# Two row buffers, raw rows for the router, and a new order on all engines

## The reference

```python
# attention by Fourier transforms, per sequence
n = layernorm(x)
s = sigmoid(norm(n)); for _ in range(10): s = 3.9 * s * (1 - s)
q = n * (1 + 0.1 * (s - 0.5)) * (1 + 0.1 * wave)
Q, K, V = q @ Wq.T + bq, mem @ Wk.T + bk, mem @ Wv.T + bv     # mem = context * constant
QKV = hamilton(hamilton(fft(Q) * filt, fft(K) * filt), fft(V) * filt)
x = x + ifft(QKV).real
# mixture of experts, top 1 of 8, capacity 1024 each
t = _layer_norm(layernorm(x), ln_gamma, ln_beta)              # a second norm inside
logits = t @ gate_weight.T
e = argmax(logits); weight = softmax(logits)[e]; rank = count of earlier tokens with the same e
x = x + layernorm(x) + weight * (gelu(t @ wi[e]) @ wo[e])     # the last term only where rank < 1024
```

## Time and profile before

| | |
|---|---|
| median of three runs | 3796.45 us (3789.59 to 3796.98) |
| profiled execution, span | 3811.8 us; the page gives no other time for it |
| TensorE busy | 3526.2 us (93%) |
| VectorE busy | 2585.9 us (68%) |
| ScalarE busy | 1623.2 us (43%) |
| GpSimd busy | 1367.9 us (36%) |
| first stage | 0 to 2357 us |

### The profile page before, as it was taken

How to read it: one execution, slowest core, us unless ns; L and a number is a source line. 1 busy time by engine, 2 the same in 40 slices (tenths; PEclk the granted TensorE clock), 3 DMA queues, 4 the chain that set the end, 5 groups by cost and what they waited for, 6 DMA issues and landing times. The chain is left out here.

```text
span 3811.8 us, 50226 instructions
## 1 busy us (share of the span) xinstructions
PE 3526.2 (93%) x15048; PEld 2654.4 (70%) x15048; DVE 2585.9 (68%) x4270; ACT 1623.2 (43%) x2726; POOL 1367.9 (36%) x2985
## 2 busy tenths in 40 slices
PE   6999998998999989989999985999999999999998
PEld 4666666666666666666666653888888888888886
DVE  5888888878888888888888883444444444444443
ACT  4445445535445445445445433333333333333332
POOL 5654654654655645555556541000000000000000
PEclk8999999999999999999999995999999999999999
DMA  6321211121111211211211102333333333333321
GB/s 213 127 97 44 80 64 44 67 77 44 71 62 44 87 58 44 97 58 44 78 67 44 67 34 78 110 105 129 121 112 122 111 122 111 111 103 108 121 101 45
DMA packets 223355, 326.29 MB, mean 86 GB/s; under 512 B 36832, under 2 KB 102624, under 8 KB 223232
## 3 DMA queue, kind: packets, MB, share of 16 engines
q1 hardware_dynamic: 207904, 307.97, 23.4%
q0 software_dynamic: 15360, 16.99, 1.3%
HBM read 256.82 MB, written 101.97 MB: 94 GB/s over the span
## 5 line engine op out<-in xcount | busy, mean ns | idle before, releaser
L1257 ACT ACTIVATE act<-hid_ps 128x512 f32<-128x512 f32 x256 | 153.3, 599 | 802.1 <-PE hid_ps L1188 802.1
L1149 POOL TENSOR_TENSOR tally<-tally,unit 1x1 f32<-1x1 f32 x16 | 2.9, 180 | 1356.7 <-DVE mixed L1330 1356.7
L403 PE MATMUL pair<-w_q,q_spec 128*128 128x512 f32 x1024 | 480.3, 619 | 0.8 <-ACT q_spec L570 0.8
L1318 DVE CAST act_h<-act 128x512 fp32r<-128x512 f32 x256 | 109.4, 428 | 527.8 <-ACT act L1257 527.8
L1188 PE MATMUL hid_ps<-tok_h,w_h 128*128 128x512 f32 x1024 | 406.0, 397 | 2.5 <-DVE tok_l L1306 2.3
L1188 PE MATMUL hid_ps<-tok_l,w_h 128*128 128x512 f32 x1024 | 399.9, 391 | 0.0
L1188 PE MATMUL hid_ps<-tok_h,w_l 128*128 128x512 f32 x1024 | 399.4, 390 | 0.0
L1204 PE MATMUL out_ps<-w_l,act_h 128*128 128x512 f32 x1024 | 398.5, 389 | 0.0
L1202 PE MATMUL out_ps<-w_h,act_h 128*128 128x512 f32 x1024 | 398.3, 389 | 0.0
L1203 PE MATMUL out_ps<-w_h,act_l 128*128 128x512 f32 x1024 | 398.3, 389 | 0.0
L1312 DVE TENSOR_TENSOR w_l<-w_raw,w_h 128x2048 fp32r<-128x2048 f32 x128 | 293.4, 2293 | 90.4 <-ACT w_h L1251 90.4
(11 more groups left out here) (174 smaller groups left out, 8116.2 us busy)
## 6 DMA issues: line engine op xcount, KB each, us to landing
w_raw<-in_L_ffn_wi SPq DMA_DIRECT2D x128, 512.0 KB, 3.4
w_raw<-in_L_ffn_wo SPq DMA_DIRECT2D x128, 512.0 KB, 4.9
w_raw<-in_x SPq DMA_DIRECT2D x32, 1024.0 KB, 5.3
w_raw<-in_ctx SPq DMA_DIRECT2D x32, 1024.0 KB, 7.3
x_res<-in_x SPq DMA_DIRECT2D x31, 1024.0 KB, 5.2
out<-x_res SPq DMA_DIRECT2D x31, 1024.0 KB, 4.2
slots<-x_tok SPq DMA_DIRECT2D x4, 4160.0 KB, 20.5
got<-slots SPq DMA_DIRECT2D x16, 1040.0 KB, 7.5
```

The source lines that it names most:

```text
L403: last = nc.tensor.matmul(pair[k % 2][:, s, :], spec[:, c, tile * 256 + s * P:tile * 256 + (s + 1) * P], w[:, c, :], start=(c == 0 and n = ...
L1149: nc.gpsimd.tensor_tensor(tally[:], tally[:], unit[:], ALU.add).then_inc(tallied, 1)
L1257: nc.scalar.activation(act32[i % 2][:], hid_ps[i % 2][:], ACT.Gelu).then_inc(gelu, 1)
L1318: v.tensor_copy(act_h[i % 4][:], act32[i % 2][:]).then_inc(ah_ready, 1)
```

## The change

1. `rows` and `slot_i` become two buffers each (p = 0 and 1 by the parity of b), with two scatter semaphores. `x_tok` and the step `tokens` go.
2. Since p must be known when the program is written, the loops of TensorE, ScalarE, GpSimd and VectorE take two sequences a turn (SyncE's does not).
3. The router turns the raw `rows`. The gate has its column mean taken out (`gate_m`, in the set-up), so that a row's own mean drops out of the product, and the row's scale (number DIM + 2 of the row) is multiplied onto the logits in `choose`, as one more step.
4. The order changes on all four engines. The turn of tile t waits for the adds of that tile, not for the norm's scales. 

```diff
-            rows = sb("rows", [P, ROWT, ROW])
-            x_tok = sb("x_tok", [P, ROWT, DIM])
+            rows = [sb(f"rows{i}", [P, ROWT, ROW]) for i in (0, 1)]
+            empty = rows[1][:, 0:1, :]
-            slot_i = sb("slot_i", [P, ROWT], i32)
+            slot_i = [sb(f"slot_i{i}", [P, ROWT], i32) for i in (0, 1)]
+            TILE_DONE = (3, 7, 4, 8)
...
TensorE
-                    def turn(b, t, f1_done):
-                        pe.wait_ge(tok_ready, b * 4 + t + 1)
+                    def turn(b, p, t, f1_done):
+                        pe.wait_ge(unfold, b * UNF + TILE_DONE[t])
...
+                    for c in range(CB):
+                        last = nc.tensor.matmul(odd_ps[:, 0:EXPERTS], ones32, gate_g[:, c, :], start=(c == 0), stop=(c == CB - 1))
...
-                    def batch(b, back, ahead):
+                    def batch(b, p, back, ahead):
                         project(b, 3)
                         if back:
                             inverse(b - 1, 0)
                         project(b, 4)
                         if back:
                             inverse(b - 1, 1)
+                        project(b, 5)
                         if ahead:
                             dft(b + 1, c_fold, cf_ready, 0)
                             dft(b + 1, q_fold, qf_ready, 4)
-                        project(b, 5)
...
-                            project(b + 2, 1)
+                            project(b + 2, 1, (0,))
                         if back:
                             logits(b, 2)
                             logits(b, 3)
                         if ahead:
+                            project(b + 2, 1, (1,))
                             project(b + 2, 2)
...
+                    with pe.Fori(3, BATCH - 3, 2) as b:
+                        batch(b, 1, True, True)
+                        batch(b + 1, 0, True, True)
...
ScalarE (the order in a batch before, and after)
-  q_of(b+1); real_parts 2, 3, 4 of b; spectra_c(b+1) with sum_x(b+2); sum_x2(b-1);
-  spectra_q(b+1) with square_x2(b-1) and square_x(b+2); real_parts 5; tokens(b-1); token_blocks 0, 1;
-  context_high(b+1); real_parts 0 of b+1; token_blocks 2, 3; base_of(b-1); real_parts 1; exps
+                        real_parts(b, 2)
+                        real_parts(b, 3)
+                        if ahead:
+                            q_of(b + 1)
+                        real_parts(b, 4)
+                        if back:
+                            sums_x2(b - 1, 1 - p)
+                        real_parts(b, 5)
+                        if ahead:
+                            spectra_c(b + 1, *([(square_x2, b - 1, 1 - p)] if back else []))
+                            context_high(b + 1)
+                            spectra_q(b + 1, *([(sum_x, b + 2)] if ahead2 else []))
+                        else:
+                            squares_x2(b - 1, 1 - p)
+                        if ahead2:
+                            squares_x(b + 2)
+  (then as before: token_blocks 0, 1; real_parts 0; token_blocks 2, 3; base_of; real_parts 1; exps)
...
GpSimd
-                        if ahead:
-                            mean1(b + 1)
                         if router:
                             mean2(b - 2)
-                            stats2(b - 2)
+                            stats2(b - 2, p)
                         if ahead:
+                            mean1(b + 1)
                             stats1(b + 1)
...
VectorE
-                            wait(dve, scattered, b * 64)
-                            wait(dve, base_ready, b * 4)
-                        lo, hi = rows[:, t, 0:DIM], rows[:, t + 2, 0:DIM]
+                            wait(dve, scattered[p], (b - p) * 32)
+                            wait(dve, base_ready, (b - 1) * 4)
+                            if p:
+                                dve.wait_ge(slots_clear, 64)
+                        lo, hi = rows[p][:, t, 0:DIM], rows[p][:, t + 2, 0:DIM]
...
+                        dve.wait_ge(stat2, b * STAT2 + STAT2)
...
+                        a2 = rows[p][:, :, DIM + 2:DIM + 3]
+                        ro.step(v.tensor_tensor(logit[:], lg, a2.broadcast_to([P, ROWT, EXPERTS]), ALU.mult)); ro.wait()
+                        ro.step(v.tensor_tensor(logit[:], logit[:], <gate_c, broadcast>, ALU.add)); ro.wait()
...
-  convert 2; folds_q(b+1); add_attended(b-1, 0); hamilton 2; convert 3; add_attended(b-1, 1); back_to_parts 0;
-  convert 4; hamilton 4; folds_c(b+2); convert 5; hamilton 5 with context_low(b+1) inside; convert 0 of b+1;
-  back_to_parts 1; convert 1 of b+1; choose(b-1); first product of b+1 with place(b-1) inside
+                        convert(b, 2)
+                        hamilton(b, 2)
+                        if back:
+                            add_attended(b - 1, 1 - p, 0)
+                        convert(b, 3)
+                        if ahead:
+                            folds_q(b + 1)
+                        convert(b, 4)
+                        if back:
+                            add_attended(b - 1, 1 - p, 1)
                         wait(dve, inv_mm, b * 4)
                         back_to_parts(b, 0)
-                        convert(b, 4)
                         hamilton(b, 4)
+                        convert(b, 5)
+                        hamilton(b, 5)
+                        back_to_parts(b, 1)
+                        hc.end()
+                        if ahead:
+                            context_low(b + 1)
                         if ahead2:
                             folds_c(b + 2)
...
                         if ahead:
                             convert(b + 1, 0)
+                        if back:
+                            choose(b - 1, 1 - p)
                         if ahead:
                             convert(b + 1, 1)
+                            first_product(b + 1, (lambda: place(b - 1, 1 - p)) if back else None)
```

More of the change, by code:

```diff
@@ L546, in square_x, with sum_x2, square_x2 @@
                         square_sum(b, t, x_in, neg1, square1, (stat1, b * STAT1 + 1), sums1, unused[0])
[L548 to L557, removed]
+                    def sum_x2(b, p, t):
+                        row_sum(b, t, rows[p], sum2, (unfold, b * UNF + UNF), (stat2, b * STAT2), sums2, unused[1])
+                    def square_x2(b, p, t):
+                        square_sum(b, t, rows[p], neg2, square2, (stat2, b * STAT2 + 1), sums2, unused[1])
                     def q_of(b):
@@ L570, in spectra @@
                             nc.scalar.activation(spec[:, u, :], xt_ps[u % 2][:], ACT.Copy).then_inc(f1_ev, 1)
-                            for step, b_ in between:
-                                step(b_, u)
+                            for step, *of in between:
+                                step(*of, u)
                     def context_high(b):
@@ L587, in real_parts, with base_of @@
                         nc.scalar.activation(re_buf[k % 2][:], pair[k % 2][:, 0, :], ACT.Copy).then_inc(re_ready, 1)
-                    def tokens(b):
+                    def base_of(b, p):
                         act.wait_ge(stat2, b * STAT2 + STAT2)
-                        wait(act, logit_mm, b * 4)
-                        act.wait_ge(slots_clear, 64)
                         for t in range(ROWT):
[L594 to L603, removed]
+                            nc.scalar.activation(residual(b)[:, t, :], rows[p][:, t, 0:DIM], ACT.Identity,
+                                                 bias=rows[p][:, t, DIM + 5:DIM + 6],
+                                                 scale=rows[p][:, t, DIM + 4:DIM + 5]).then_inc(base_ready, 1)
                     def token_blocks(b, tiles):
@@ L623, in spectra_q, with sums_x, squares_x, sums_x2 @@
                         spectra(b, q_spec, 4, (f2_mm, b * 6 - 2), between)
-                    all_tiles(0, sum_x, square_x)
+                    def sums_x(b):
+                        for t in range(ROWT):
+                            sum_x(b, t)
+                    def squares_x(b):
+                        for t in range(ROWT):
+                            square_x(b, t)
+                    def sums_x2(b, p):
+                        for t in range(ROWT):
+                            sum_x2(b, p, t)
+                    def squares_x2(b, p):
+                        for t in range(ROWT):
+                            square_x2(b, p, t)
+                    sums_x(0)
+                    squares_x(0)
                     spectra_c(0)
@@ L725, in stats1, with stats2 @@
                         c.end()
-                    def stats2(b):
+                    def stats2(b, p):
                         c = s2c
```

181 lines of the change are left out of this document (87 added, 94 removed).

## The result

The changed kernel takes **3757.9 us** (median of 4 runs, 3753.1 to 3759.0); the kernel before, run beside it, took 3793.4 (3789.6 to 3797.0). The ratio is 0.9886, interval 0.9858 to 0.9913: 35.5 us gained where 122 were forecast. 3757.9 lies outside the range of 3615 to 3722.

The account below looks back on a forecast made before the run. Bound: the ring of waits, with inverse 1 behind add 0 behind hamilton 2. 41.87 + 24.84 = 66.7 us per batch, plus 0.7 for clock, 67.4; 103 plus 19 at the end, 122 off 3796.5, gives 3674 us; range 3615 to 3722.

Parts of the forecast that it names:

- 66.7 us at full clock: First stage, per batch: TensorE's 41.87 us plus 24.84 from real-row copy to first add, without slow clock.
- 67.4 us per batch: First stage: 66.7 us plus 0.7 for a slow-clock loss of 1.4 us taken in half the batches.
- the price of nothing for the doubled loops: Loops unrolled by two: the forecast time held no instruction-fetch cost; such stalls appeared only in rivals.
- Rivals 1 and 2: Slow clock behind inverse 1 in every batch, 21 us more, 3695 (0.15); VectorE fetch stall, 35 us, 3709 (0.12).
- Rival 2: VectorE's branch back, on the ring: a fetch stall of about 2.5 us per pass, 35 us, 3709; chance 0.12.
- hamilton 2: VectorE's product, now ahead of the first add: 8.63 us of the 24.84 leading to inverse 1.
- The experts' loop fetches without a wait at its seam: Argument against rival 2: the experts' loop fetches instructions on each pass, yet shows no wait at its branch.
- Rival 5: VectorE's doubled body, 34 KB in four 8 KB pieces, refetched each pass: 11.6 us, 3836, slower; chance 0.07.
- the ring: First stage's closed chain of waits through TensorE and VectorE, from inverse 1 to the next: 66.7 us per batch.
- The q_spec waits: TensorE waits for q spectra: 0.7 us in front of the q-product, 0.3 inside dft q, 1.0 together.
- Rivals 3, 4 and 5: TensorE bounds at 63.8, 3566 (0.07); scatter wait only moves, 3796 (0.06); whole VectorE body refetched, 3836 (0.07).
- the 5.8 us wait goes: VectorE's wait per batch for the previous rows' scatter, before the first add, vanishes with two rows buffers.

Follow-up runs that it names:

- the mend of the third: Changed kernel with conversion 3 and the first add ahead of hamilton 2, plus ScalarE's row sums put behind the c spectra: 4014.7 us, ratio 1.0566.
- the early add: Changed kernel with conversion 3 and the first add ahead of hamilton 2: 3780.9 us; with VectorE's loop also written out: 3753.5 us.
- the versions of the old order: Changed kernel, old orders, q_of behind real part 2, folds_q behind first add, VectorE's loop written out: 3579.1 us; x's squares also behind the q spectra: 3561.7 us.

## Why the prediction was wrong

**Where the 122 us went.** Between the two profiled executions lie 3811.8 - 3756.6 = 55.2 us: 30 x (70.84 - 69.68) = 34.8 by the batches (103 forecast), 1551.6 - 1525.7 = 25.9 behind the first add of sequence 30 (19 forecast), and 5.5 lost before the first batch (0 forecast). The profiled execution of before lay 17 us above the median of its runs, 3796.45 (its span of 3811.8 against runs whose spans are 1.8 below their times), that of after at its median. The forecast was taken off the median, as if after's execution would lie as high, so these 17 us are part of the miss: 68 + 5.5 - 7 + 17 = 84 = 3758 - 3674. The 68 are the step to explain.

**The step that failed** is the one from "66.7 us at full clock" to "67.4 us per batch", and the price of nothing for the doubled loops. Rivals 1 and 2, weighed at 0.15 and 0.12 and taken one at a time, came together:
- *Clock.* "I take it in half of the batches, 0.7." Each batch had its slow stretch and lost 1.6 to 2.1 us by it. The wait that decides was laid out at 2.9 us and called in between; it was 3.3 to 5.1, and with VectorE's loop written out, at 3.1, each batch still had its stretch. Measured alone: 45 us, for the 21 allowed.
- *Fetch.* Rival 2 put 2.5 us per pass on VectorE's branch. The trace shows 1.7 to 2.0 us of idle there, and writing the loop out gives 3.2 per pass, 41.5 us, since hamilton 2 and the slow stretch grow behind it and the written-out steps are shorter. "The experts' loop fetches without a wait at its seam" was true of TensorE; I carried it to VectorE, which no row covered. Rival 5's size of the body does not hold either: written out, VectorE brings one packet of 8 KB per batch (24 in 1700 us), where 236 instructions at 71 bytes (131072/1840; the working has 73) would bring two.

Together they are 30 x (69.68 - 67.21) = 74 us, of which 21 were in the forecast: 53 of the 68. The other 15 are the ring itself, 67.21 measured at full clock and without the branch where 66.7 were laid out. The Trainium skill, "Runtime: NRT & Kernel Launch", section "Instruction fetch mechanics", says that a branch taken to a page not held stalls until it is fetched; this case agrees, for VectorE's body of two batches (1.67 us idle, packets on q14) and not for its body of one (neither, before and with one buffer).

**What held.** The ring, to 0.5 us a batch. Of its terms, hamilton 2 was low, 8.96 (1037.35 to 1046.31) and 9.32 in place of 8.63, which also makes the wait at inverse 1 longer: it now runs beside GpSimd's real bins. The q_spec waits, 0.8 and 0.2 for 0.7 and 0.3. No scatter wait, none for x_tok; VectorE waits for the logits and real part 1, and also, which was not forecast, for real part 0 (34 waits for real parts in 17 batches). Slow stretches only at inverse 1. Rivals 3, 4 and 5 fell: TensorE is not the bound, no other wait took over the 5.8 us whole, and the fetch is far from 11.6 us a pass.

**What the working did not ask.** It gave the gain to the second buffer ("the 5.8 us wait goes") and took the new order as given. Both runs with one buffer show that wait gone too, in either order, once the turns read raw rows; in the old order 110 us of gain are that part's. The new order gives 109 us back, because it puts hamilton 2 ahead of three things: the first add (inverse 1), conversion 3 (project 5), and the last of the rows (ScalarE's sums and, behind them, the c spectra). I had named the first as the bound, rightly, but as the only one. Taken away one after the other, each gave way to the next, and the mend of the third met a fourth, GpSimd's mean. In the old order conversion 3 is behind hamilton 2 as well, but project 5 stands behind both dfts there and does not wait; the 22.0/18 = 1.2 us of that trace stand in front of project 4, for conversion 2. That the order as a whole costs 109 us is shown. How it splits among the four engines is not: the orders were not put back one by one.

## What to carry to other kernels

Price the parts of a change apart, the new order too: here one part held 110 of the 148 us of gain, another gave 109 back, and the second buffer was worth 38 us in one order and -21 in the other. Before moving a product in an in-order queue, list everything queued behind it and who waits for each; freeing one waiter alone only shows the next. And a cost set at nothing because another engine bears it without a wait holds for that engine only: 1.9 us of idle on the ring came back as 3.2, with a longer product and a longer stretch of slow clock behind it.

## What the runs showed of the hardware

- A loop on VectorE of two batches (472 instructions by the working's count) is fetched again on every pass: about 5 packets of 8 KB on q14, three of them around the branch, and 1.7 to 2.0 us of idle there. Writing it out gave 41.5 us over 13 passes (27 with the early add), shorter steps included; in the versions of the old order 18 and 13 us. The body of one batch shows neither, in before and in the new order with one buffer.
- Waits of 3.1 and 3.3 us on TensorE were followed by about 1.5 and 1.7 us lost at the 1.2 GHz level in each batch. With one of 4.95 us the stretch was twice as long but began within the wait, and 2.1 us were lost. 12 matmuls nobody reads, put into the wait, brought 45 us.
- VectorE's products of 512 columns last longer beside some of GpSimd's work. While GpSimd multiplied the real bins (968.9 to 974.6 us) they were recorded at 0.73 to 0.88 us; beside its scatter (962.4 to 968.1), its stats1 steps and its idle time at 0.68 to 0.69. The whole product took 8.96 to 9.32 us for the 8.63 taken from before.
